# Pairs of heads on the tensor engine, a new order of keys and values, and the expert gate's tanh folded into the expert weights

## What is computed

```python
x = x + tanh(g_xattn[0]) * attention(layernorm(x), ctx)     # 16 heads of 64, causal, with a mask
h   = rmsnorm(layernorm(x), gamma1)                         # "mix": attention among the 16 heads of one token
q   = (h @ Wq + bq).reshape(b, t, H, HD)                    # H = 16, HD = 16
kv  = ((h @ Wdown + bdown) @ Wup + bup).reshape(b, t, H, 2 * HD)
k, v = split(kv, 2, axis=-1)
att = softmax(einsum('bthd,btgd->bthg', q, k) / sqrt(HD))
y   = n + einsum('bthg,btgd->bthd', att, v).reshape(b, t, D) @ Wo + bo
h2  = rmsnorm(y, gamma2)
gate = softmax(h2 @ Wg + bg)                                # 8 experts
out = y + einsum('btd,edf,bte->btf', h2, We, gate)          # "experts"
x = x + tanh(g_ffn[0]) * out
```

## Time and profile before

| | value |
|---|---|
| median of three runs | 2798.7 us |
| profiled execution | 2801.4 us |
| its span, first to last instruction | 2799.6 us |
| PE busy | 2515.2 us, 90% |
| DVE busy | 1772.2 us, 63% |
| ACT busy | 1268.1 us, 45% |
| POOL busy | 958.5 us, 34% |
| mean granted clock of PE | 0.957 |

### The profile page before, as it was taken

One profiled execution on the slowest core, in us unless ns is written; L12 is line 12 of the kernel. 1 busy time (PEld: TensorE's weight loads), 2 busy tenths in 40 slices (PEclk: granted clock), 3 DMA queues, 4 the chain that ended last, 5 costly groups with the idle time before them and its releaser, 6 DMA issues. The chain is left out here.

```text
span 2799.6 us, 48038 instructions
## 1 busy us (share of the span) xinstructions
PE 2515.2 (90%) x16128; PEld 2056.0 (73%) x16128; DVE 1772.2 (63%) x3970; ACT 1268.1 (45%) x3939; POOL 958.5 (34%) x878
## 2 busy tenths in 40 slices
PE   6989999999999999999845699999999999999998
PEld 5767777777777777777635477777787777777877
DVE  3488888888788888888873544445444444444541
ACT  5644555445554456545402344444443433444441
POOL 1344544444444454443441223233222222232320
PEclk9999999999999999999956899999999999999999
DMA  4000000000000000000004000000000000000000
GB/s 138 13 5 16 13 4 15 15 15 12 4 15 15 15 12 4 15 15 8 5 4 153 8 9 13 15 15 15 15 15 15 15 15 4 11 15 15 15 8 8
DMA packets 25857, 51.67 MB, mean 18 GB/s; under 512 B 6272, under 2 KB 7040, under 8 KB 24640
## 3 DMA queue, kind: packets, MB, share of 16 engines
q1 hardware_dynamic: 25792, 50.84, 5.5%
HBM read 42.44 MB, written 8.39 MB: 18 GB/s over the span
## 5 line engine op out<-in xcount | busy, mean ns | idle before, releaser
L1147 POOL TENSOR_SCALAR l_probs<-l_probs,l_rinv 128x256 f32<-128x256 f32 x512 | 238.6, 481 | 589.9 <-DVE l_rinv L1362 588.3
L1258 ACT ACTIVATE l_probs<-l_score,l_negmax 128x256 f32<-128x256 f32 x512 | 238.9, 473 | 264.7 <-DVE l_negmax L1357 264.7
L1562 PE MATMUL l_ffn<-l_w,l_hid 128*128 128x256 f32 x1536 | 347.5, 381 | 1.0 <-ACT l_hid L1232 1.0
L318 POOL TENSOR_TENSOR l_prod<-l_q,l_kv 128x2048 f32<-128x2048 f32 x64 | 289.5, 4536 | 170.6 <-DVE l_att L580 92.7
L1562 PEld LDWEIGHTS l_ffn<-l_w,l_hid 128*128 128x128 f32 x1536 | 287.2, 190 | 50.5 <-issue 13.9
L332 POOL TENSOR_TENSOR l_prod<-l_att,l_kv 128x2048 f32<-128x2048 f32 x32 | 178.9, 5590 | 305.4 <-DVE l_att L597 178.1
L1369 DVE COPY l_probsT<-l_attn 128x512 f32<-128x512 f32 x256 | 175.6, 686 | 159.5 <-PE l_attn L1525 159.5
L677 DVE CUSTOM_DVE_ANT_0 l_probs<-l_score,l_mbias 128x256 f32<-128x256 f32 (+1 forms) x512 | 161.7, 353 | 118.5 <-PE l_score L872 91.2
L606 DVE TENSOR_TENSOR l_prod<-l_att,l_kv 128x2048 f32<-128x2048 f32 x32 | 217.6, 6799 | 3.4
L1357 DVE TENSOR_REDUCE l_negmax<-l_score 128x2 f32<-128x512 f32 x256 | 175.1, 684 | 65.5 <-PE l_score L1513 65.5
L404 ACT ACTIVATE l_probs<-l_probs,l_negmax 128x256 f32<-128x256 f32 x256 | 130.7, 511 | 186.5 <-DVE l_negmax L677 183.4
(11 more groups left out here) (267 smaller groups left out, 7510.1 us busy)
## 6 DMA issues: line engine op xcount, KB each, us to landing
l_ctxin<-in_ctx SPq DMA_DIRECT2D x32, 256.0 KB, 3.1
l_xin<-in_x SPq DMA_DIRECT2D x16, 256.0 KB, 2.7
l_x<-in_x SPq DMA_DIRECT2D x16, 256.0 KB, 2.6
x<-l_acc SPq DMA_DIRECT2D x16, 256.0 KB, 2.0
l_xin<-x SPq DMA_DIRECT2D x16, 256.0 KB, 3.2
l_x<-x SPq DMA_DIRECT2D x16, 256.0 KB, 2.7
out<-l_x SPq DMA_DIRECT2D x16, 256.0 KB, 2.0
l_hid<-in_w SPq DMA_DIRECT2D x2, 1536.0 KB, 8.8
```

Source lines behind the costliest of these rows:

```text
L318: nc.gpsimd.tensor_tensor(prod[:, u].rearrange("p (h g d) -> p h g d", h=half, g=H), q4[:, u * half:(u + 1) * half].unsqueeze(2).to_broadc ...
L1147: last = nc.gpsimd.tensor_scalar(probs[:, j % 4, t * S:(t + 1) * S], probs[:, j % 4, t * S:(t + 1) * S], rinv[:, j, t:t + 1], 1.0, ALU.mul ...
L1258: last = nc.scalar.activation(probs[:, s % 4, t * S:(t + 1) * S], ps[:, t * S:(t + 1) * S], ACT.Exp, bias=negmax[:, s, t:t + 1], accum_out ...
L1562: last = T.matmul(ps[:, 0:D], hid[:, c, t * P:(t + 1) * P], w2[:, c, :], start=c == 0, stop=c == 3 * NHC - 1)
```

## The change

All of it is in layer 0 and in the arrangement of the inputs.

- PE issues the scores of heads j and j + 1 together in even steps, alternating between the two halves of the array's rows, and waits for both score banks first. It issues the value products of heads j and j + 1 together in odd steps from 5 on, alternating between halves of the columns.
- The maximum of an odd head j from 5 on now waits for the transposes of head j - 4. `probsT` has three buffers; `pos` is gone, the mask is made in mbias.
- The columns of Wup and bup are put in another order: all keys first, then all values with the feature index outside. The key and value views of kv follow.
- The factor tanh(g_ffn[0]) is multiplied into the expert weights when they are split into high and low parts. The gate is no longer multiplied by it; DVE only inverts the sum, and ACT scales the two halves of the gate at its step 7.
- The sums of experts 0, 1 and 2 move from steps 6, 7, 8 to 7, 8, 9 on DVE. PE's products stay where they were.

```diff
-LAG_V1 = 5
+LAG_V0 = LAG_V1 = 5
...
+        add_at = {7: 0, 8: 1, 9: 2, 10: 3, 12: 4, 14: 5, 15: 6, 17: 7}
...
-                    k4 = kv[:, t].rearrange("p (g two d) -> p g two d", two=2, d=HD)[:, :, 0, :]
+                    k4 = kv[:, t, 0:D].rearrange("p (g d) -> p g d", d=HD)
...
-                    v4 = kv[:, 0].rearrange("p (g two d) -> p two d g", two=2, d=HD)[:, 1]
+                    v4 = kv[:, 0, D:2 * D].rearrange("p (d g) -> p d g", d=HD)
...
+                    if k >= NS_EXPERTS:
+                        nc.scalar.activation(hi, stage[0:rows, k % 2, 0:src.shape[1]], ACT.Copy, scale=tg[:, 1:2]).then_inc(split_hi, 1)
...
-                    if j >= 2:
-                        act.wait_ge(pv_done, H * a + j - 1)
-                    nc.scalar.copy(probsT[:, j % 2, :], ps[:, 0:CAUSAL]).then_inc(free, 1)
+                    if j >= 3:
+                        act.wait_ge(pv_done, H * a + j - 2)
+                    nc.scalar.copy(probsT[:, j % 3, :], ps[:, 0:CAUSAL]).then_inc(free, 1)
...
+                    if c is not None and s == 6:
+                        act.wait_ge(gsum_ready, c + 1)
+                        for t in range(NT):
+                            last = nc.scalar.activation(gate[:, t], gate[:, t], ACT.Copy, scale=gsum[:, t:t + 1])
+                        last.then_inc(gate_ready, 1)
...
-                    V.reciprocal(gsum[:], gsum[:])
-                    dve.drain()
-                    V.tensor_scalar(gsum[:], gsum[:], tg[:, 1:2], None, ALU.mult)
-                    dve.drain()
-                    V.tensor_tensor(gate[:], gate[:], gsum[:].unsqueeze(2).to_broadcast([P, NT, E]), ALU.mult)
-                    dve.drain()
+                    V.reciprocal(gsum[:], gsum[:]).then_inc(gsum_ready, 1)
...
+                    if j == 0:
+                        dve.wait_ge(gate_ready, c + 1)
...
+                    if j >= 4 and j % 2 == 1:
+                        _, transposed, _, when = attn.at(f"T{j - 4}", a)
+                        wait_apart(dve, dve_passed, transposed, when)
...
+                def pair_scores(a, j):
...
+                    pe.wait_ge(free0, turn0)
+                    pe.wait_ge(free1, turn1)
+                    T.matmul(ps0[:, 0:S], qT[rows0, c, P:S], kT[rows0, c, :], start=True, stop=True)
+                    T.matmul(ps1[:, 0:S], qT[rows1, c, P:S], kT[rows1, c, :], start=True, stop=True)
+                    T.matmul(ps0[:, S:CAUSAL], qT[rows0, c, 0:P], kT[rows0, c, 0:P], start=True, stop=True).then_inc(full0, 1)
+                    T.matmul(ps1[:, S:CAUSAL], qT[rows1, c, 0:P], kT[rows1, c, 0:P], start=True, stop=True).then_inc(full1, 1)
...
+                def pair_values(a, j):
...
+                    both_emptied(pe, attn, f"T{j}", f"T{j + 1}", a)
...
+                    T.matmul(ps[rows0, u * S:(u + 1) * S], v[:, 0, m0], p0[:, 0:S], start=True, stop=False)
+                    T.matmul(ps[rows1, u * S:(u + 1) * S], v[:, 0, m1], p1[:, 0:S], start=True, stop=False)
+                    T.matmul(ps[rows0, u * S + P:(u + 1) * S], v[:, 1, m0], p0[:, S:CAUSAL], start=False, stop=True).then_inc(pv_done, 1)
+                    T.matmul(ps[rows1, u * S + P:(u + 1) * S], v[:, 1, m1], p1[:, S:CAUSAL], start=False, stop=True).then_inc(pv_done, 1)
```

More of the change, by code:

```diff
@@ L145, in layer0 @@
         qT, kT, v = sb("qT", [P, NC0, S]), sb("kT", [P, NC0, S]), sb("v", [P, NT, INNER])
-        pos, mbias = sb("pos", [P, S]), sb("mbias", [P, CAUSAL])
-        probs, probsT = sb("probs", [P, 4, CAUSAL]), sb("probsT", [P, 2, CAUSAL])
+        mbias = sb("mbias", [P, CAUSAL])
+        probs, probsT = sb("probs", [P, 4, CAUSAL]), sb("probsT", [P, 3, CAUSAL])
         negmax, rsum, rinv = sb("negmax", [P, H, NT]), sb("rsum", [P, H, NT]), sb("rinv", [P, H, NT])
@@ L210, in layer0 @@
                   piece(ins["we"][:, 1, :], (we[0][:, 1, :], we[1][:, 1, :]))]
-        NS, NS_FIRST = len(splits), 3
+        NS, NS_FIRST, NS_EXPERTS = len(splits), 3, len(splits) - 2
         params = [(bo[:], ins["bo"].to_broadcast([P, D])),
@@ L374, in split @@
                     act.wait_ge(raw_in[k % 2], 16 * (k // 2 + 1))
-                    nc.scalar.copy(hi, stage[0:rows, k % 2, 0:src.shape[1]]).then_inc(split_hi, 1)
+                    if k >= NS_EXPERTS:
+                        nc.scalar.activation(hi, stage[0:rows, k % 2, 0:src.shape[1]], ACT.Copy, scale=tg[:, 1:2]).then_inc(split_hi, 1)
+                    else:
+                        nc.scalar.copy(hi, stage[0:rows, k % 2, 0:src.shape[1]]).then_inc(split_hi, 1)
                 for k in range(NS_FIRST):
@@ L753, in split @@
                     dve.wait_ge(split_hi, k + 1)
-                    V.tensor_sub(lo, stage[0:rows, k % 2, 0:src.shape[1]], hi.bitcast(F32)).then_inc(split_lo, 1)
+                    raw = stage[0:rows, k % 2, 0:src.shape[1]]
+                    if k >= NS_EXPERTS:
+                        V.scalar_tensor_tensor(out=lo, in0=raw, scalar=tg[:, 1:2], in1=hi.bitcast(F32), op0=ALU.mult,
+                                               op1=ALU.subtract).then_inc(split_lo, 1)
+                    else:
+                        V.tensor_sub(lo, raw, hi.bitcast(F32)).then_inc(split_lo, 1)
                 def mix_gather_ready(b, u):
@@ L956, in body @@
                     for s in range(STEPS):
-                        if a is not None and s < H:
+                        if a is not None and s < H and s % 2 == 0:
                             if s % 4 == 0 and s > 0:
@@ L961, in body @@
                                 attn.emptied(pe, "k3", a)
-                            head_scores(a, s)
+                            pair_scores(a, s)
                         if a is not None and s == LAG_T:
@@ L1660, in twice, with keys_then_values @@
         return np.concatenate([w, w], axis=-2).reshape(*w.shape[:-3], NC1 * P)
+    def keys_then_values(w):
+        w = w.reshape(*w.shape[:-1], H, 2, HD)
+        keys, values = w[..., 0, :], np.swapaxes(w[..., 1, :], -1, -2)
+        return np.concatenate([keys.reshape(*w.shape[:-3], D), values.reshape(*w.shape[:-3], D)], axis=-1)
     spread = np.zeros((H, SLOT, D), np.float32)
```

59 lines of the change are left out of this document (28 added, 31 removed).

## The result

The changed kernel takes 2709.6 us (median, 2706.6 to 2711.1) where the kernel before takes 2799.0 on the same chip: 0.968 of its time, 95% interval 0.966 to 0.970. The forecast was 2660 with a range of 2610 to 2718: the direction and the range held, the size did not, since 89 us were saved instead of 138. The profiled execution took 2711.1 and has a span of 2709.3, against 2799.6. From the first product of layer 1 to the end the two traces take 1289.1 and 1288.5 us, so nearly all of it lies in layer 0, as expected.

The account below looks back on a forecast made before the run. DVE was taken to decide the end of a batch's middle and last stretches, after a first stretch of waits in turns. 13 batches x 8.3 = 108, plus 30 elsewhere, gave 138 us saved: 2660 us, range 2610 to 2718.

Parts of the forecast that it names:

- step 5: Keys first, values transposed: v is read at a step of 1, so each of two weighings a batch ends 2.4 us earlier.
- The rival that the step costs little: Weighings: v's step costs little or another lock replaces it; 3.5 us a batch saved, 2731 us; chance 0.12.
- step 3: Gate: DVE loses a 3.85 us multiplication and about 0.3 of work, ACT's scalings cost nothing; -4.15 us a batch.
- steps 1, 2, 7: Pairs cut PE's work 13.2 us a batch, as capacity; first stretch gains 0.4, DVE's idle time in the middle falls 1.3.
- Step 7: Middle of the batch: of DVE's 4.9 us idle, 1.3 goes; the chain maximum, exp, xT high, xT low stays.
- A: First stretch of a steady batch, 621.57 to 640.09, a chain in turns; forecast gain 0.4 of 18.5 us.
- step 4: Middle of the batch: new DVE wait for head 3's transposes, +1.0 us, and xn's normalisation blocked by POOL, +1.3.
- step 6: Score pairs 12 and 14: PE waits for both banks, about 3 us before 14, 1.3 before 12; costs nothing.
- a rival, with a chance of 0.04: Clock rival: more idle places on PE lower the granted clock and make the kernel slower; chance 0.04.
- 8.3 forecast: Saving in us per steady batch: 0.4 in its first stretch, 5.5 in the middle, 2.4 in the last.
- a forecast of 30: Saving outside the 13 steady batches: first batch 9 us, second 6, last with heads 8, drain 7.
- a chance of 0.11 to the contrary: Rival: halves of 64 don't overlap, PE keeps its 81 us of work a batch, 2700 us; chance 0.11.

## Why the prediction was right in direction and wrong in size

- **Order of keys and values** (step 5). Right, and all of the gain. POOL 4.54 (forecast 4.52), DVE behind it 2.15 (2.29, a figure that the prediction calls DVE's product and that is a subtraction of the same size), 2.7 and 2.6 to 3.0 for 2.4 in each of the two stages. The rival that the step costs little fell. The change from 5.60 to 4.54 is a factor of 1.23, as the query-key row had it (1.24).
- **The gate** (step 3) is the step that failed. Its 3.85 is gone, as written, but "-4.15" was booked as time. It was time of DVE, and PE's scores 7 and ACT's part of xT come no sooner for it: alone and on top of the order it gives 0.0 a batch, with the pairs 0.1. Step 7 said that "the chain maximum, exp, xT high, xT low stays", yet took the whole gain through it.
- **The pairs** (steps 1, 2, 7). The overlap is there, and the work fell by 9.2 us a batch (79.09 to 69.88 between the kernel with order and gate and the changed one). The forecast was 13.2; a part of the difference is that a dip's slower matmuls (0.41 for 0.28) count as busy. "Capacity, not time" held, apart from 2.1 in the undipped stage 6-12 (23.1 to 21.0), which the prediction had given to the gate. In A they give 0.1 (0.4).
- **What comes late instead** (step 4). The wait for the transposes of head 3 came at its size, 1.25 for 1.0. The xn block did not come, since 1.6 of waits for exp and gate stood in front of it. The sum of 2.3 became 2.85, by other items, so its size is luck.
- **Pair waits** (step 6). PE stands 2.16 before pair 14 and costs DVE nothing by itself; but the list ended there. k1's wait of 1.82 for the bank of xT was missing.
- **The granted clock** is the term that was missing from the sum. It stood only as a rival, with a chance of 0.04. What that rival named is there: more idle time of PE, 5.8 to 11.9 us a batch, and more time at the lower level, 5.8 to 8.4. Its size stays below the gain: in the changed kernel k1 has a dip in each of 13 batches (1.4), stage 0-6 in 5 of them (1.5), the last stage in 7 of them (1.3): 18.2 + 7.5 + 9.1 = 35 us, where the dips of the kernel before cost some 6. Without them a batch takes 79.1, and 86.6 before: 7.5 saved for 8.3 forecast. The kernel with the waits filled shows those 79.1. That 7.5 comes so near to 8.3 is luck in part: in stage 6-12 the prediction had 3.15 from the gate's -4.15, the +2.3 and the -1.3 of steps 4 and 7, and the 2.1 that came are the pairs', which it had put at nothing there.
- **Ends.** First batch 64.4 for 67.8, second 76.5 for 82.6, last and drain together 12.3 shorter: 22 for a forecast of 30. The first batch misses most, 3.4 for 9: PE was busy 64.60 of 67.80 there, but the pairs didn't pass on there either. Even the 3.4 is not clear: with the gate alone, which has no part in the first batch, that batch takes 64.8.

Together: 13 x 5.2 + 22 = 90, for 138. Of the missing 48, 29 are the clock (35 - 6), 8 the ends, 10 the 0.8 a batch by which the steps at full clock were too high.

What stays open: whether the wait for the transposes of head 3 costs anything. A kernel with a fifth buffer of the probabilities was to remove it (1 us a batch, 2690 to 2700 expected), but it needs more on-chip memory than there is: 512 bytes of a partition are left where its last tensor takes 2048. So there is no time for it. And why a dip falls in one batch and not in the next with the same instructions: I can say what shifts them, not foretell them.

## What to carry to other kernels

Two engines that wait for each other in turns have to be costed as a loop: before booking a removed operation as time, follow DVE to the next place where it waits for PE or ACT, and book only what is still there behind it. Making an engine's work shorter can make its waits longer (PE's idle time went from 5.8 to 11.9 us a batch here), and such a wait can have a price of its own, as the 1.82 us before k1 with a clock of 0.59 in the 3.6 us behind it; read the granted clock by stretch and ask whether it falls in slack or on the path. If on the path, remove the wait, or fill it with matmuls that nobody reads, and look where the next dip goes, because filling a wait in slack made the kernel before slower, 2799.0 to 2820.2.

## What the hardware showed that I had not expected

- Added matmuls that nobody reads made a kernel faster: 24 a batch, 79.42 / 13 = 6.1 us of PE's busy time, 2709.6 to 2682.7. The same remedy in the kernel before made it slower, 2799 to 2820.
- Short waits were enough here. Behind one of 1.82 us, with none over 0.52 in the 20 us before it, the clock was at 0.59 for 3.6 us, and every one of the 13 batches has this dip. Not every such wait has one: with order and gate alone PE waits up to 1.4 us for DVE's last gather and 0.8 for transposes in each batch, at a clock of 1.00. In the changed kernel 8.4 us a batch are at the lower level with no wait over 2.8 in PE's list.
- The lower level can last while PE is fully busy: 10.20 of 10.20 us at 0.50, with pairs and 8-column matmuls at its beginning.
- Value products whose two halves share all rows of the array and differ in columns run at the same time (both start at 519.73, 0.80 a pair): what layer 1 shows for strips of 32 holds for halves of 64, where the prediction had left a chance of 0.11 to the contrary.
